# TensorE alternates quarters of one tile's second layer with chunks of another tile's first layer

## The reference, cut to what matters

```python
x = x + xattn(ctx, layernorm(x))                  # dynamic-time-warping alignment, x: (4, 512, 128)
xf = layernorm(x).reshape(2048, 128)              # H = 128, I = 512, E = 8 experts, K = 2
scores = sigmoid(xf @ gate_w + bias)
top_scores, top_idx = top_k(scores, 2)            # each token goes to two experts
w = scatter(top_scores / (sum + 1e-6))
up   = einsum('th,ehi->tei', xf, up_w) + up_b     # first layer
hact = gelu(up)
eo   = einsum('tei,eih->teh', hact, down_w) + down_b   # second layer
combined = einsum('teh,te->th', eo * 0.1, w)
shared = (gelu(xf @ sw_up + sb_up) @ sw_down + sb_down) * 0.1
out = shared + combined;  x = x + out / (max|out| + 1e-6)
```

## Time and profile before

| | us |
|---|---|
| median of 3 runs (266.03 to 267.21) | 266.16 |
| the profiled execution's own time | 266.78 |
| its span, first to last instruction | 264.9 |
| expert loop, first matmul of `up(0)` to last of `down(22)` | 174.72 to 242.75 |
| one tile of that loop in its steady part | 2.87 |
| PE busy over the span | 171.1 (65%) |

### The profile page before, as it was taken

How to read it: one execution, slowest core, us unless ns; L and a number is a source line. 1 busy time by engine, 2 the same in 40 slices (tenths; PEclk the granted TensorE clock), 3 DMA queues, 4 the chain that set the end, 5 groups by cost and what they waited for, 6 DMA issues and landing times.

```text
span 264.9 us, 5441 instructions
## 1 busy us (share of the span) xinstructions
PE 171.1 (65%) x1351; PEld 113.8 (43%) x1352; DVE 198.2 (75%) x941; ACT 139.9 (53%) x336; POOL 110.2 (42%) x169
## 2 busy tenths in 40 slices
PE   1492029999000001465645978979999999998991
PEld 0240014443000000363322323359999999997640
DVE  2853899999994492588779799779888888883045
ACT  5552027993000402308997666567888788874031
POOL 8400040000000001462277878874777777777200
PEclk9998558999755555555557899999999999999999
DMA  6002969530403000000112144343433322000355
GB/s 195 26 1 95 117 210 333 175 52 4 84 1 66 28 0 0 4 2 0 45 56 70 45 146 144 100 133 93 126 95 95 105 84 83 28 16 2 109 208 158
DMA packets 34562, 22.08 MB, mean 83 GB/s; under 512 B 15251, under 2 KB 30577, under 8 KB 34533
## 3 DMA queue, kind: packets, MB, share of 16 engines
q1 hardware_dynamic: 31062, 16.18, 23.9%
q0 software_dynamic: 2496, 4.24, 4.9%
q10 hardware_dynamic: 975, 1.33, 1.5%
HBM read 12.57 MB, written 9.03 MB: 82 GB/s over the span
## 4 chain that ended last, share of the span: by engine, by line
PE 37%; DVE 33%; POOL 8%; ACT 6%; DMA 6%; issue 6%; DVEq 1%; SPq 1%; ACTq 0%; POOLq 0%
PE bank L1052 8%; PE bank L1053 7%; DVE arena_b L1225 7%; PE bank L1054 7%; POOL sorted_dram L700 7%; DVE edge L1216 4%; DVE arena_f L1220 3%; DVE arena_c L1217 3%; PE bank L1162 3%; ACT x_sb L825 2%; DVE arena_f L1227 2%; PE bank L1105 2%; PE bank L949 2%; PE bank L985 1%; POOL row_and_place L708 1%
## 5 line engine op out<-in xcount | busy, mean ns | idle before, releaser
L735 POOL DMA_INDIRECT expert_dram<-arena_d,arena_f x46 | 49.4, 1074 | 18.5 <-issue 15.7
L897 ACT ACTIVATE arena_f<-bank,tile_bias 128x256 f32<-128x256 f32 x92 | 35.9, 474 | 1.3 <-PE bank L1054 0.6
L1052 PE MATMUL bank<-arena_a,up_hi 128*128 128x256 f16 (+1 forms) x108 | 32.7, 302 | 4.6 <-ACT x L814 2.2
L1052 PE MATMUL bank<-down_hi,arena_d 128*128 x184 | 32.5, 219 | 1.3 <-DVE arena_g L1525 1.3
L1525 DVE TENSOR_TENSOR arena_g<-arena_f,arena_d 128x512 f16<-128x512 f32 x46 | 32.0, 695 | 1.6
L1053 PE MATMUL bank<-arena_a,up_hi 128*128 128x256 f16 (+1 forms) x108 | 32.4, 300 | 0.0
L1054 PE MATMUL bank<-arena_a,up_lo 128*128 128x256 f16 (+1 forms) x108 | 32.4, 300 | 0.0
L1054 PE MATMUL bank<-down_hi,arena_g 128*128 x184 | 32.3, 219 | 0.0
L1053 PE MATMUL bank<-down_lo,arena_d 128*128 x184 | 32.3, 219 | 0.0
L673 POOL COPY met_at<-arena_b 32x3 f16 (+1 forms) x26 | 3.9, 181 | 66.6 <-DVE arena_b L1285 62.4
L985 PE MATMUL bank<-arena_b,minus_one 128*128 (+1 forms) x26 | 3.9, 184 | 42.6 <-issue 42.6
(11 more groups left out here) (258 smaller groups left out, 466.9 us busy)
## 6 DMA issues: line engine op xcount, KB each, us to landing
arena_f<-sorted_dram SPq DMA_DIRECT2D x23, 130.0 KB, 2.2
arena_d<-in_L_ffn_up_w SPq DMA_DIRECT2D x6, 256.0 KB, 5.7
arena_d<-in_L_ffn_down_w SPq DMA_DIRECT2D x5, 256.0 KB, 5.7
sorted_dram<-padding SPq DMA_DIRECT2D x9, 130.0 KB
x_sb<-in_x SPq DMA_DIRECT2D x4, 256.0 KB, 4.4
arena_c<-row_and_place SPq DMA_DIRECT2D x4, 256.0 KB, 2.8
arena_b<-expert_dram SPq DMA_DIRECT2D x4, 256.0 KB, 4.6
arena_c<-expert_dram ACTq DMA_DIRECT2D x4, 256.0 KB, 5.0
```

Source lines behind the costliest of these rows:

```text
L735: pool.indirect_dma_start(out=expert_dram.ap(), in_=y_row[:, j % Y_SLOTS, n, :], in_offset=None, out_offset=bass.IndirectOffsetOnAxis(ap=p ...
L897: last = act.activation(hid[:, k, m, cols], banks[UP_BANK + HALVES * k + m][:, cols], ACT.Gelu, bias=bias, scale=1.0 / WSCALE)
L1052: pe.matmul(o, a_hi, b_hi, start=start, stop=False)
```

## The change

PE no longer does all of `down(j-2)` and then all of `up(j)`. It alternates quarters of the one with chunks of the other: `down_part(j-2, s)` has part n = s // 2 and half m = s % 2, two groups, and `up_part(j, s)` one group; `turn(j+2)` moves from the end of the tile to its middle. The tile's register is loaded at the head of the iteration. `hid_hi`, `hid_lo` and `xT` get three homes (`HOMES`), and so does the column register. `down_part` has a new wait, `y_row_ready`, for the PSUM bank that it overwrites. ACT does `gelu(j)` before `y_copy(j-2)`, and DVE does `keep_turned(j+2)` before `hid_halves(j)`.

```diff
-        hid_hi, at = within(arena_d, TILES * H, (SLOTS, HALVES, I * PARTS // HALVES), F16)
+        hid_hi, at = within(arena_d, TILES * H, (HOMES, HALVES, I * PARTS // HALVES), F16)
...
             for j in range(EXPERT_TILES + SLOTS):
+                if j < EXPERT_TILES:
+                    gelu(j, j % SLOTS)
                 if j >= SLOTS:
                     y_copy(j - SLOTS)
-                if j < EXPERT_TILES:
-                    gelu(j, j % SLOTS)
...
-            column_reg = [pe.alloc_register(f"column{k}") for k in range(SLOTS)]
+            column_reg = [pe.alloc_register(f"column{i}") for i in range(HOMES)]
+
+            def column(j):
+                return pe.snap(column_reg[j % HOMES], min_val=0, max_val=(E - 1) * I)
...
+            def up_part(j, c):
+
+                k, x = j % SLOTS, xT[:, j % HOMES]
+                m, q = c // (NCH // HALVES), c % (NCH // HALVES)
+                o = banks[UP_BANK + HALVES * k + m][:, q * ET:(q + 1) * ET]
+                w = bass.ds(column(j) + c * P, P)
+                mm = three_passes(o, up_hi[:, w], up_lo[:, w], x[:, 0:ET], x[:, ET:2 * ET], True, True)
+                if q == NCH // HALVES - 1:
                     mm.then_inc(up_done, 1)
...
+            def down_part(j, s):
+
+                k, i = j % SLOTS, j % HOMES
+                n, m = s // HALVES, s % HALVES
+                if s == 0 and j >= SLOTS:
+                    pe.wait_ge(y_row_ready, j - SLOTS + 1)
+                if n == 0:
+                    pe.wait_ge(hid_ready, j * HALVES + m + 1)
+                for q in range(NCH // HALVES):
+                    c = m * (NCH // HALVES) + q
+                    w = bass.ds(column(j) + c * P, P)
+                    h = slice(q * ET + n * P, q * ET + (n + 1) * P)
+                    mm = three_passes(banks[Y_BANKS[k]][:, n * H:(n + 1) * H], hid_hi[:, i, m, h], hid_lo[:, i, m, h],
+                                      down_hi[:, w], down_lo[:, w], c == 0, c == NCH - 1)
+                if s == NCH - 1:
+                    mm.then_inc(y_done, 1)
...
             for j in range(EXPERT_TILES + SLOTS):
-                if j >= SLOTS:
-                    down(j - SLOTS, j % SLOTS)
                 if j == 1:
                     pe.wait_ge(accT_ready, B)
                 if j < EXPERT_TILES:
-                    up(j, j % SLOTS)
-                if j + SLOTS < EXPERT_TILES:
-                    turn(j + SLOTS, j % SLOTS)
+                    pe.reg_load(column_reg[j % HOMES], tile_column[j:j + 1, 0:1])
+                for s in range(NCH):
+                    if j >= SLOTS:
+                        down_part(j - SLOTS, s)
+                    if j < EXPERT_TILES:
+                        if s == 0:
+                            pe.wait_ge(xT_by_act if j % 2 else xT_by_dve, j // 2 + 1)
+                        up_part(j, s)
+                    if s == NCH // HALVES - 1 and j + SLOTS < EXPERT_TILES:
+                        turn(j + SLOTS, j % SLOTS)
...
             for j in range(EXPERT_TILES):
-                hid_halves(j, j % SLOTS)
                 if j + SLOTS < EXPERT_TILES and j % 2 == 0:
                     keep_turned(j + SLOTS, j % SLOTS)
+                hid_halves(j, j % SLOTS)
```

More of the change, by code:

```diff
@@ L61 @@
 SLOTS = 2
+HOMES = 3
 Y_SLOTS = 4
@@ L250, in build @@
         S_LAST = at
-        xT, at = within(arena_a, TILES * P, (SLOTS, HALVES * ET), F16)
+        xT, at = within(arena_a, TILES * P, (HOMES, HALVES * ET), F16)
         x_row, at = within(arena_f, B * S, (ROW_HOMES, PARTS * (H + 2)))
         x_row = x_row.rearrange("p k (n d) -> p k n d", n=PARTS)
-        hid_lo, at = within(arena_g, 0, (SLOTS, HALVES, I * PARTS // HALVES), F16)
+        hid_lo, at = within(arena_g, 0, (HOMES, HALVES, I * PARTS // HALVES), F16)
         shared_g, at = within(arena_g, at, (2, S))
@@ L888, in keep_turned @@
                 act.wait_ge(xT_in_psum, j + 1)
-                act.activation(xT[:, k, :], banks[XT_BANKS[k]][:], ACT.Copy).then_inc(xT_by_act, 1)
+                act.activation(xT[:, j % HOMES, :], banks[XT_BANKS[k]][:], ACT.Copy).then_inc(xT_by_act, 1)
             def gelu(j, k):
@@ L1108, in turn @@
                 mm.then_inc(xT_in_psum, 1)
[L1110 to L1120, removed]
-                    mm.then_inc(up_done, 1)
@@ L1123, in down @@
[L1123 to L1135, removed]
+            def up_part(j, c):
[5 more added lines that the diff above has]
+                if q == NCH // HALVES - 1:
+                    mm.then_inc(up_done, 1)
@@ L1517, in keep_turned @@
                 dve.wait_ge(xT_in_psum, j + 1)
-                dve.tensor_copy(xT[:, k, :], banks[XT_BANKS[k]][:]).then_inc(xT_by_dve, 1)
+                dve.tensor_copy(xT[:, j % HOMES, :], banks[XT_BANKS[k]][:]).then_inc(xT_by_dve, 1)
             def hid_halves(j, k):
+                i = j % HOMES
                 for m in range(HALVES):
                     dve.wait_ge(gelu_done, j * HALVES + (m + 1))
-                    dve.tensor_copy(hid_hi[:, k, m, :], hid[:, k, m, :]).then_inc(hid_hi_ready, 1)
+                    dve.tensor_copy(hid_hi[:, i, m, :], hid[:, k, m, :]).then_inc(hid_hi_ready, 1)
                     dve.wait_ge(hid_hi_ready, j * HALVES + (m + 1))
-                    dve.tensor_tensor(hid_lo[:, k, m, :], hid[:, k, m, :], hid_hi[:, k, m, :], ALU.subtract
+                    dve.tensor_tensor(hid_lo[:, i, m, :], hid[:, k, m, :], hid_hi[:, i, m, :], ALU.subtract
                                       ).then_inc(hid_ready, 1)
```

## The result

The changed kernel takes 283.2 us, median of 4 runs (281.88 to 283.79); beside it the kernel before took 266.69 us (266.03 to 267.3). The ratio is 1.061, with a 95% interval of 1.056 to 1.066. The forecast was 277.1 us (274.3 to 280.0): the sign and the bound were right, and the size was 6.1 us too small, outside the range and 1.1 us above the upper end of my likeliest case (282.1).

What follows compares the result with a forecast made beforehand. PE's matmuls bind now (2.87 us a tile); afterwards its sequencer would: 61.4 groups, 9.1 and 0.2 heads, 1.0 fetches make 71.8 against 61.02, 10.8 more. With 0.1 at the start, 266.16 + 10.9 = 277.1 us (274.3 to 280.0).

Steps and rivals of the forecast that it cites:

- likeliest case: In the expert loop PE's sequencer becomes the bound: 277.1 us, between 274.0 and 282.1; chance 0.90.
- register work is free: Rival: register work runs beside the loop's matmuls and the tile stays at 2.87 us; 265.9 us, chance 0.04.
- partly hidden: Rival: cheaper register work in the loop, 0.21 us a group, 3.00 a tile; 268.8 us, chance 0.03.
- The fifth case, the lower clock: Rival: in the loop the granted clock falls to 1.2 GHz, a tile needs 5.7 us; 323 us, chance 0.01.
- Register work: All 12 groups of a loop tile carry address instructions at 0.24 us each; 256 groups make 61.4 us.
- Load and wait: Head of each iteration, TENSOR_LOAD to first address instruction: 0.48 us, 19 times, 9.1 us; two waits without load, 0.2.
- The estimate from the Trainium skill's floor: About 600 ns for each of the loop's 19 register loads would cost 5.6 us more, giving 282.7 us.
- Starved fetches: Occasional groups in the loop take 0.37 us instead of 0.24: 0.13 us 8 times, 1.0 us, ends 0 and 2.
- New waits: In the loop, `y_row_ready` ahead of `down(j)`'s first quarter costs nothing beyond its instruction; the third homes cost nothing.
- The end: After the loop, 9.8 us of matmuls cover the DRAM results and move along, so all 10.8 + 0.1 reaches the end.
- The start: Before the steady loop little moves: iteration 3 begins at 181.85, 0.1 us later than in the kernel before.

Runs made afterwards that it cites:

- e1_reuse: Changed kernel with the second layer's weight addresses computed for n = 0 and reused for n = 1; 268.93 us, 1.006 times the kernel before.
- e2_before_regs: Kernel before in its old order, with each second-layer group computing its weight address anew, so all 12 groups carry register work; 282.22 us, 1.056.
- e12_two_passes: Changed kernel with the third product of every group left out, 24 matmuls a tile instead of 36; 283.01 us, 1.063 times the kernel before.
- e9_late_turn: Kernel of e1_reuse with `turn` at the end of the iteration again; 268.9 us, 1.005 times the kernel before.
- e4_few_loads: Changed kernel with only the first 3 of the 23 register loads, all other register work kept; 277.95 us, 1.038 times the kernel before.
- e3_static: Changed kernel with weight columns known at build time and no register work or load in the loop; 268.92 us, 1.006 times the kernel before.
- e5_late_turn: Kernel of e1_reuse with `turn` at the end of the iteration again, on another chip; 298.09 us beside 292.95 for the kernel before (1.019).

## Why the prediction was right and wrong

**The bound: right.** "The sequencer becomes the bound" was the likeliest case, and e1_reuse, e2_before_regs and e12_two_passes show it from three sides. The rival "register work is free" fell with e2, and "partly hidden" with the pitch of 0.244. The Trainium skill's rule behind the former (Advanced Engine Details and Errata, section Sequencer Loop: other instructions can be read and queued while a control instruction executes) holds here only as far as the queue reaches: 8 groups of register work a tile were hidden, 12 were not. The fifth case, the lower clock, did not come: the granted clock was 1.00 through the loop. (The slices that I named for it begin with PE at five tenths, slice 22 of the earlier trace rows, and not at seven.)

**Register work: right, slightly short.** 0.24 us a group was forecast, 0.244 measured: 62.5 in place of 61.4 us.

**Load and wait: right.** 0.48 was forecast for a head, 0.471 measured. Taking one load out gave 0.39. The estimate from the Trainium skill's floor of 600 ns for the load (DMA: Bandwidth & Descriptors, section Latency and other measured facts), 282.7 us, came close to the measured 283.2 only by accident, since the load took 0.308 us here as before.

**Starved fetches: the step that failed.** "I don't know how often this comes", I wrote, and took 0.13 us eight times, 1.0 us in all, with 2 us as the upper end. It was 4.1 us: about 0.2 us in every tile, three or four short steps of 0.03 to 0.155. The kernel before held the evidence, and the earlier trace rows has one such step (0.37 for 0.24). I took the one instance for a rare event, since the queue of matmuls ahead of PE hides all others there. This term alone is 3.1 us of the 6 that were missing.

**New waits: a second miss.** The earlier `turn` is not among the new waits that I went through, so it stood in the sum at nothing, without a reason. PE now asks for the rows of tile 5 in the middle of iteration 3, and the sequencer stands for 0.85 us until they have landed at 183.7. The other new wait, `y_row_ready`, was rightly priced at nothing: the waits of PE in the loop show none on ACT. The rows come late because they are read after the last scatter into the sorted rows (POOL starts it at 177.9, it lands at 180.9, then comes the load). In the old order the turn came at the end of the iteration (184.38 for tile 5), and nothing showed this wait. e9_late_turn, with the old place, has it no more.

**The end: a third miss.** "That cover moves along with the loop's end" assumed that the scatters keep their distance to the loop. They did not: ACT now copies tile 20's result behind the Gelu of tile 22, and the last iterations are short, so POOL's six scatters end 1.7 us later after the loop. The 9.8 us of cover was just too short, which cost 1.2 us of waiting and 1.5 in all. I had named the ACT order and priced it by the steady tile alone.

**The start:** iteration 3 was forecast 0.1 us later and began 0.3 us earlier. Counted from the loop's first matmul (174.33, before 174.72) it is 0.1 us later, as forecast; the loop itself began 0.4 us sooner, although the change leaves what runs ahead of it as it was. That part of the sum is luck.

The sum: 1.1 (groups) - 0.1 (heads) + 3.1 (short steps) + 0.85 (rows) - 0.4 (start) + 1.5 (end) = 6.05 us, which is, within rounding, the gap between the forecast span of 264.9 + 10.9 = 275.8 and the measured 281.8.

## What to carry to other kernels

An engine's sequencer has a budget of its own, and bare instructions behind the ones with register work are its slack: before reordering, count the sequencer's time per tile, and keep what is computed once in registers across the new order. When slack turns into a bound, everything that the queue used to hide comes to light at once, so look for rare odd steps in the trace of before where the engine had just run dry, and ask how often they come per instruction, not per sighting. And price a moved step at the first and last iterations apart from the steady one: that is where rows are not there yet and where queues of other engines must drain.

## What the runs showed of the hardware

- A joined register instruction and a single one together cost PE's sequencer 0.244 us, with two or with three matmuls in the group (e12_two_passes and the changed kernel). A register load from SBUF cost 0.39 us of the tile, for a record of 0.308.
- Once no queue of matmuls covers it, PE's sequencer loses about 0.45 us in some 256 instructions (a matmul with its weight load counted as two), in steps about 32 instructions apart (the changed kernel, e12_two_passes, e4_few_loads). Why is not shown.
- After 2.3 us without a matmul the granted clock fell to its lower level for most of 4 us, and 16 sums took 8.83 in place of 7.15 us (e3_static). After 1.6 us of idle time in e1_reuse and 1.2 us in the changed kernel it stayed at the upper level.
- The kernel before took 267 us on one chip and 293 on another, where the trace of e5_late_turn shows DVE and ACT standing repeatedly for up to 3 us without a releaser on this core.
